# Cross attention on one core: output rows dealt over four steps, value chunks in a ring of four

## The reference, cut to what matters

```python
x = x + attn(layernorm(x))
h = layernorm(x)
q = (h @ Wq).reshape(B, 112, 16, 128)
k = (ctx @ Wk).reshape(B, 375, 8, 128)
v = (ctx @ Wv).reshape(B, 375, 8, 128)
p = softmax(where(mask, q k^T / sqrt(128), -inf))
x = x + (p v).reshape(B, 112, 2048) @ Wo
x = x + ffn(layernorm(x))
```

## Time and profile before

| | |
|---|---|
| Median of 3 runs | 2684.8 us (2684.68 to 2687.51) |
| The profiled execution | 2685.35 us, span 2683.7 us |
| TensorE matmuls (PE) | 2482.7 us busy, 93% |
| TensorE weight loads (PEld) | 2257.6 us, 84% |
| VectorE (DVE) | 1733.0 us, 65% |
| ScalarE (ACT) | 1241.2 us, 46% |
| GpSimd (POOL) | 1030.1 us, 38% |
| Mean granted TensorE clock | 0.957 |

### The profile page before, as it was taken

The page is one execution under the profiler, slowest core; times in us unless marked ns, Lnnn a source line. Parts: engine busy times, 40 slices in busy tenths (PEclk is TensorE's granted clock), DMA queues, the critical chain, the costliest instruction groups (busy, mean ns, idle before and its releaser), DMA issues. The chain is left out here.

```text
span 2683.7 us, 46237 instructions
## 1 busy us (share of the span) xinstructions
PE 2482.7 (93%) x14850; PEld 2257.6 (84%) x14851; DVE 1733.0 (65%) x4899; ACT 1241.2 (46%) x3183; POOL 1030.1 (38%) x1424
## 2 busy tenths in 40 slices
PE   6899897799999999999999999999999999979488
PEld 5888886788989898889989898898989888869376
DVE  7878886565575657566575756656565665644466
ACT  4555553454454545445454545445454454522211
POOL 4334443243343434334353534334343343431422
PEclk9999998899999999999999999999999999975699
DMA  8322332412122112212121211111111111122654
GB/s 256 95 71 84 96 108 89 162 50 66 62 75 66 62 54 74 74 52 83 52 91 58 88 55 53 54 41 55 51 57 54 53 55 41 41 72 70 220 178 129
DMA packets 108892, 217.87 MB, mean 81 GB/s; under 512 B 20336, under 2 KB 48720, under 8 KB 108416
## 3 DMA queue, kind: packets, MB, share of 16 engines
q1 hardware_dynamic: 103440, 188.42, 21.9%
q0 software_dynamic: 5040, 16.58, 1.7%
q10 hardware_dynamic: 224, 10.49, 1.2%
HBM read 134.57 MB, written 91.36 MB: 84 GB/s over the span
## 5 line engine op out<-in xcount | busy, mean ns | idle before, releaser
L1171 POOL TENSOR_SCALAR x_probs<-x_probs,x_inv 112x376 f32<-112x376 f32 x512 | 639.3, 1258 | 273.6 <-DVE x_inv L1323 273.6
L1165 POOL TENSOR_SCALAR x_bias<-x_top 112x1 f32<-112x1 f32 x512 | 129.1, 252 | 871.8 <-DVE x_top L1295 864.9
L1215 ACT ACTIVATE x_probs<-x_probs,x_bias 112x376 f32<-112x376 f32 x512 | 307.0, 603 | 105.2 <-POOL x_bias L1165 104.7
L1380 PE MATMUL x_ps_o<-x_pT,x_v 128*128 128x224 f32 (+1 forms) x2304 | 310.3, 279 | 43.2 <-DVE x_pT L1302 42.5
L1380 PEld LDWEIGHTS x_ps_o<-x_pT,x_v 128*128 128x128 f32 (+1 forms) x2304 | 288.0, 192 | 69.6 <-DVE x_pT L1302 61.5
L1380 PE MATMUL x_ps_f<-x_xT,x_wq 128*128 128x448 f32 x1536 | 339.3, 371 | 4.5 <-issue 4.5
L1380 PE MATMUL x_ps_f<-x_wo,x_oT 128*128 128x512 f32 x1344 | 315.7, 391 | 1.0 <-DVE x_oT L1311 1.0
L1380 PE MATMUL x_ps_s<-x_kT,x_qT 128*112 128x376 f32 x1536 | 314.6, 340 | 1.5 <-DVE x_top L1295 1.5
L1380 PE MATMUL x_ps_f<-x_ctxT,x_wk 128*128 128x376 f32 x1536 | 306.4, 335 | 1.9 <-DVE x_ctxT L1272 1.9
L1380 PEld LDWEIGHTS x_ps_f<-x_xT,x_wq 128*128 128x128 f32 x1536 | 282.4, 189 | 26.5 <-issue 4.7
L1380 PEld LDWEIGHTS x_ps_f<-x_wo,x_oT 128*128 128x128 f32 x1344 | 252.6, 189 | 50.0 <-issue 1.2
(11 more groups left out here) (186 smaller groups left out, 3799.5 us busy)
## 6 DMA issues: line engine op xcount, KB each, us to landing
x_ctxs<-x_ctxT SPq DMA_DIRECT2D x32, 752.0 KB, 3.8
x_ctxT<-x_ctxs SPq DMA_DIRECT2D x32, 752.0 KB, 4.3
x_xT<-h2T SPq DMA_DIRECT2D x16, 896.0 KB, 5.0
m_rows<-slots SPq DMA_DIRECT2D x35, 258.0 KB, 3.0
slots<-w_blank SPq DMA_DIRECT2D x8, 1032.0 KB, 5.2
x_ctxn<-in_ctx_dram SPq DMA_DIRECT2D x32, 256.0 KB
m_hn<-in_L_ffn_W_dram SPq DMA_DIRECT2D x32, 256.0 KB
w_xa<-in_x_dram SPq DMA_DIRECT2D x32, 224.0 KB, 3.3
```

What stands on the lines that cost most here:

```text
L1165: pool.tensor_scalar(bias[:, m:m + 1], top[:, m:m + 1], -0.1 * NEG, -SCALE, ALU.max, ALU.mult) \
L1171: pool.tensor_scalar(probs[0:T, m, 0:SE], probs[0:T, m, 0:SE], inv[:, m:m + 1], None, ALU.mult).then_inc(normed, 1)
L1215: act.activation(probs[0:T, m, 0:SE], probs[0:T, m, 0:SE], ACT.Exp, bias=bias[:, m:m + 1], scale=SCALE, accum_out=total[:, m:m + 1]).then_ ...
L1380: last = pe.matmul(out, w, r, start=m == 0, stop=m == len(jobs) - 1)
```

## The change

The output rows leave `ORDER`. They get a bank of their own, `ps_r`, taken from the fills, which now have two. A tile's eight heads are multiplied in four parts (`ROWS_AT`: 3, 1, 3 and 1 heads at g=2 and g=3 of the batch where the tile is due and at g=0 and g=1 of the next); VectorE adds the tile after the last part. `oT` holds three tiles instead of two. V's first chunk moves to g=3 of the batch before, which takes a ring of four chunk slots for `v`; the context of b+2 is transposed half at g=2, half at g=3, behind P·V. x pieces go to g=1 and g=2 of batches 1 and 2 of a quad. Weights of keys are kept for one half only, in pieces by head. The context as loaded and the raw mask have one buffer instead of two. On ScalarE and VectorE the exponentials and inverses now come ahead of the early fills, and mask row, x piece and weight piece go to the end of a step.

```diff
+    VRING = NKC + 1
...
-    RING = 2 * P
+    RING = 3 * P
...
-        out = [("K", b + 1, g)] if b + 1 < NB else []
-        if g == 3 and b + 2 < B:
-            out += [("C", b + 2, 0), ("C", b + 2, 1)]
-        if g == 2 and b in TILE_OF:
-            out.append(("O", TILE_OF[b], 0))
-        return out
+        return [("K", b + 1, g)] if b + 1 < NB else []
 
     def late_fills(i):
         b, g = divmod(i, G)
-        out = [("V", b, c) for c in range(NKC)] if g == 1 else []
+        out = []
+        if g >= 2 and b + 2 < B:
+            out.append(("C", b + 2, g - 2))
+        if g == 3 and b + 1 < NB:
+            out.append(("V", b + 1, 0))
+        if g == 1:
+            out += [("V", b, c) for c in range(1, NKC)]
         if b % QUAD == QUAD - 1 and b + 1 < NB:
             out += [("Q", b // QUAD + 1, 2 * g + h) for h in range(2)]
         return out
 
     def before_transposes(i):
-        return late_fills(i)[:-1]
+        fs = late_fills(i)
+        return fs if fs and fs[-1][0] == "C" else fs[:-1]
 
     def behind_transposes(i):
-        return late_fills(i)[-1:]
-
-    HEAD = [("C", 0, 0), ("C", 0, 1)] + [("K", 0, g) for g in range(G)] + [("C", 1, 0), ("C", 1, 1)] + \
-           [("Q", 0, h) for h in range(H)]
-    TAIL = ("O", TILE_OF[NB], 0)
-    ORDER = HEAD + [f for i in range(STEPS) for f in early_fills(i) + late_fills(i)] + [TAIL]
+        fs = late_fills(i)
+        return [] if fs and fs[-1][0] == "C" else fs[-1:]
+
+    ROWS_AT = {2: [(0, 3)], 3: [(3, 4)], 4: [(4, 7)], 5: [(7, H)]}
+
+    def row_parts(i):
+
+        out = []
+        for back in (1, 0):
+            b, g = divmod(i, G)
+            b, g = b - back, g + G * back
+            if b in TILE_OF:
+                out += [(TILE_OF[b], h0, h1) for h0, h1 in ROWS_AT.get(g, [])]
+                if b == NB - 1 and g == G - 1:
+                    out += [(TILE_OF[b], h0, h1) for late in ROWS_AT if late > g for h0, h1 in ROWS_AT[late]]
+        return out
+
+    HEAD = [("C", 0, 0), ("C", 0, 1)] + [("K", 0, g) for g in range(G)] + [("Q", 0, h) for h in range(4)] + \
+           [("C", 1, 0), ("C", 1, 1)] + [("Q", 0, h) for h in range(4, H)] + [("V", 0, 0)]
+    ORDER = HEAD + [f for i in range(STEPS) for f in early_fills(i) + late_fills(i)]
     PLACE = {f: n for n, f in enumerate(ORDER)}
     assert len(PLACE) == len(ORDER)
-    HALVED = {f: n for n, f in enumerate([f for f in ORDER if f[0] != "O"])}
-    BANKS = 3
+    BANKS = 2
...
-    PIECES = {"k": CC, "v": CC, "q": KC, "o": H // 2}
-    FIRST_SPLITS = [("k", 0, n) for n in range(CC)], [("q", 0, n) for n in range(KC)], [("v", 0, n) for n in range(CC)]
+    PIECES = {"k": G, "v": CC, "q": KC, "o": H // 2}
...
-        if b == B - 8 and g < CC:
-            return [("k", 1, g)]
+        if 0 <= i - G * (B - 2) - 1 < G:
+            return [("k", 1, i - G * (B - 2) - 1)]
         if b == B - 3:
             return [("q", 1, g)]
-        if i == G * B:
+        if i == G * (B - 1) + 2:
             return [("v", 1, n) for n in range(CC)]
-        if b == B + 1:
-            return [("o", 1, g)]
+        if 0 <= i - G * (B + 1) - 2 < PIECES["o"]:
+            return [("o", 1, i - G * (B + 1) - 2)]
...
-        return b // QUAD + 1 if b % QUAD == 1 and b // QUAD + 1 < NB // QUAD else None
+        if b // QUAD + 1 == NB // QUAD or b % QUAD not in (1, 2) or g not in (1, 2):
+            return None
+        return b // QUAD + 1, 2 * (b % QUAD - 1) + g - 1
...
+        def v_slot(b, c):
+            return (NKC * b + c) % VRING
...
                 for b in range(NB):
-                    if b + 2 < B:
-                        load_ctx(b + 2)
-                    if b + 1 < B:
-                        keep_ctxT(b + 1)
-                    if b + 1 in TILE_OF:
-                        load_base(TILE_OF[b + 1])
+                    if b in TILE_OF:
+                        load_base(TILE_OF[b])
                     if b % QUAD == 0 and b // QUAD + 1 < NB // QUAD:
                         load_x(b // QUAD + 1)
-                    if b == B - 12:
-                        for n in range(PIECES["k"]):
-                            load_w(("k", 1, n))
                     if b == B - 4:
                         sp.wait_ge(fill_ready, until(("Q", B // QUAD - 1, H - 1)))
                         for n in range(PIECES["q"]):
                             load_w(("q", 1, n))
+                    if B <= b + 2 < NB:
+                        load_ctxT(b + 2)
                     if b == B - 1:
                         sp.wait_ge(fill_ready, until(("V", B - 1, NKC - 1)))
                         for n in range(PIECES["v"]):
                             load_w(("v", 1, n))
-                    if B <= b + 2 < NB:
-                        load_ctxT(b + 2)
+                    if b - 1 in TILE_OF:
+                        store(TILE_OF[b - 1])
+                    if b == B + 1:
+                        sp.wait_ge(rows_ready, TILES)
+                        for n in range(PIECES["o"]):
+                            load_w(("o", 1, n))
                     if b + 2 < NB:
                         load_mask(b + 2)
-                    if b in TILE_OF:
-                        store(TILE_OF[b])
-                    if b == B:
-                        sp.wait_ge(fill_ready, until(("O", TILES - 1, 0)))
-                        for n in range(PIECES["o"]):
-                            load_w(("o", 1, n))
+                    if b == B - 2:
+                        for n in range(PIECES["k"]):
+                            sp.wait_ge(fill_ready, until(("K", B - 1, n)))
+                            load_w(("k", 1, n))
+                    if b + 2 < B:
+                        keep_ctxT(b + 2)
+                    if b + 3 < B:
+                        load_ctx(b + 3)
...
+                fill(HEAD[-1])
                 for i in range(STEPS):
-                    for p in splits_at(i):
-                        split(p)
+                    exps(i)
                     for f in early_fills(i):
-                        if f[0] != "O":
-                            fill(f)
-                    exps(i)
-                    if x_piece(i) is not None:
-                        split_x(x_piece(i), i % G)
+                        fill(f)
                     if i >= 2:
                         out(i - 2)
                     for f in before_transposes(i):
...
                         probsT(i - 1)
                     for f in behind_transposes(i):
                         fill(f)
+                    if x_piece(i) is not None:
+                        split_x(*x_piece(i))
+                    for p in splits_at(i):
+                        split(p)
...
+                mask_row(0)
                 for i in range(STEPS):
-                    if i % G == 0:
-                        mask_row(i // G)
                     maxima(i)
-                    for p in splits_at(i):
-                        split(p)
+                    inverses(i)
                     for f in early_fills(i):
-                        if f[0] != "O":
-                            fill(f)
-                    inverses(i)
-                    if x_piece(i) is not None:
-                        split_x(x_piece(i), i % G)
-                    for f in early_fills(i):
-                        if f[0] == "O":
-                            add(f)
+                        fill(f)
                     if i >= 2:
                         out(i - 2)
+                    for tile, h0, h1 in row_parts(i):
+                        if h1 == H:
+                            add(tile)
                     for f in before_transposes(i):
                         fill(f)
                     if i >= 1:
                         probsT(i - 1)
                     for f in behind_transposes(i):
                         fill(f)
+                    if i % G == 1 and i // G + 1 < NB:
+                        mask_row(i // G + 1)
+                    if x_piece(i) is not None:
+                        split_x(*x_piece(i))
+                    for p in splits_at(i):
+                        split(p)
...
+                def rows(tile, h0, h1):
+                    if h0 == 0:
+                        weights("o", tile // TILES)
+                        pe.wait_ge(o_lo, G * (last_batch(tile) + 1))
+                        if tile:
+                            pe.wait_ge(rows_added, tile)
+                    slot = tile * P % RING
+                    for h in range(h0, h1):
+                        for a, b_ in PASSES:
+                            last = pe.matmul(ps_r[:], oT[:, a, h, slot:slot + P], wo[:, b_, h, :],
+                                             start=h == 0 and (a, b_) == PASSES[0],
+                                             stop=h == H - 1 and (a, b_) == PASSES[-1])
+                    if h1 == H:
+                        last.then_inc(rows_ready, 1)
...
                     scores(i)
                     for f in early_fills(i):
                         fill(f)
```

(38 more changed lines are left out.)

69 lines of the change are left out of this document (38 added, 31 removed).

## The result

The changed kernel takes 2695.2 us (median of 6 runs, 2693.7 to 2699.7) against 2684.7 us for the kernel before, measured beside it: ratio 1.0041, 95% interval 1.0029 to 1.0054. It is slower, by 10.5 us; the forecast was 5 us faster. The time lies inside the range, the direction is wrong.

What follows compares the result with a forecast made beforehand. TensorE's instruction stream, working 97 to 99% of each quad, was taken as the bound. Head +6.3, first quad +2.9, other first-half quads +0.3 and second half −14.7 gave −5.2 us: forecast 2680 us, range 2655 to 2697.

Steps and rivals of the forecast that it cites:

- (g): First quad (four batches sharing one query set): VectorE bears four `wo` pieces in short steps; 117.0 against 114.1 us, +2.9.
- (b): Keys' low part behind inverses: stored 3.2 us after m, where maxima start; steps under 5.6 us cost up to 0.55.
- The first rival: New waits do not appear: about −3.2 us a full quad, −4 with a missing tile, near 2648; chance 0.20.
- (a): Step lengths with rows dealt over four steps: 24.7 us a first-half batch, 24.1 second-half; row parts cost 0.
- (d): Full quads: 120.4 against 121.9 us in the first half (−1.5), 116.3 against 119.0 in the second (−2.7).
- (e): Quads with a missing tile: first half 118.1 against 117.1 us (+1.0), second half 113.6 against 114.4 (−0.7).
- (f): Head, ahead of the first scores: first V chunk behind `wv`'s halving, second context between query products; +6.3 us.
- (h): Second-half key weights, one buffer, loaded in batch 30: ScalarE waits for a piece; +4.5 us once.
- (i): Second half's start and end: `wo` pieces in steps without rows 0; three batches without x −1.5, last batch −3 us.
- third rival: New idle times bring low-clock stretches, at most three or four of 1 to 1.5 us each: 2684; chance 0.08.

Runs made afterwards that it cites:

- chip 1: The kernel before and the changed kernel, both unaltered, run and traced again on another chip: changed kernel's ratio to the kernel before 1.0033.
- Pieces in the gap: The changed kernel, but VectorE halves each weight piece behind the next step's maxima instead of at the step's end: ratio to the kernel before 0.9999.
- all three placements: The changed kernel with `wo` loaded ahead of mask 1, second-half `wk` pieces halved one step later, VectorE's weight pieces behind the next maxima: ratio 0.9975.

## Why the prediction was wrong

**The failing step is (g), the first quad.** It was to cost +2.9 us and costs 8.7 on chip 1, which is 5.8 of the 12.6 us between forecast and measurement there, and 7.9 in the first profile. The miss is all in batch 0: 25 us worked out, 29.7 measured (30.4 on chip 1). The sum took VectorE to be busy without a break: four cycles of 4.2 us, the V halves, context, mask and pieces by their lengths. It left out what VectorE waits for. First, the loads were taken as landed, because the sentence on SyncE closed with "each is still issued most of a batch before its use … so nothing". That holds for the loads that the change moves and not for those queued behind them: dropping the second mask buffer puts a wait for mask row 0 ahead of four `wo` loads, and VectorE stands 3.1 us. Loading them first gives 1.0 to 2.9 us back. Second, a late key holds V2's bank, and VectorE then waits another 2.2 us for V2's product. Pieces in the gap give 3.7 to 5.6 us back, all three placements 6.6 on one chip, the keys' old order beside them another 8.2 (116.1 to 107.9), of which 4.0 are in batch 0. How the 5 to 6 us that were missed divide between the load, the bank and the low clock is not shown: the single edits overlap.

**(b) was worked out rightly.** "Keys stored at m + 3.2" (3.16) holds, and the short steps' 0.55 us stand in the 4.2 us of batch 0's four cycles. What it didn't ask is whether the new order is worth having. The first rival described the kernel with the old order back, roughly: −3.2 and −4 a quad, and 119.2 and 114.5 were measured (−2.7 and −2.5); "near 2648" is a ratio of 0.986, and that run had 0.9897. It said that earlier keys would do it, not that a change of order would bring them.

**(a), (d).** An unbroken first-half batch is 24.86 us, not 24.7, and V0's wait costs 0.54, not 0.65: full quads gained 0.8 us each, not 1.5. The row parts cost nothing, as taken. In the second half (d) and (e) were right to 0.3 us over six quads together. **(e)** in the first half came out at 118.2 to 118.4 for 118.1; it cost +1.3 a quad for +1.0, since the kernel before took 116.8 to 117.1 in these quads.

**(f)**, the head, cost +6.0 and +6.9 us from the first query product on, for 6.3. That the first scores also came 6.3 us later by the clock of chip 1 is luck, as the 10.7 of the first chip shows. **(h)**, ScalarE's wait for `wk`: 4.97 us for the "4 us or more", the quad +2.2 on chip 1 and +3.7 on the first for +1.8. **(i)**: of the −3 us at the end only 0.5 came on chip 1 (1.9 on the first), and quad 9, with `wo`'s pieces, cost 1.2 and 2.9 instead of nothing.

**The clock, third rival.** TensorE's busy time in the first quad rose from 107.9 us to 110.2, although it holds twelve matmuls of output rows fewer (36 for 48, 2.0 us of busy time), which now stand in the next quad: some 4 us of work more, an estimate, at the low clock behind the new idle times, on top of 5.6 us more of idling (11.8 against 6.2). The page "TensorE: Matmul & The Clock Gate" of the Trainium skill (Part 1) says that the throttled state is the default and activity releases it; by it the forecast would have been 4 us higher, and the trace agrees with its sign and size. This rival happened, but the longest of its idle times stood in part behind a load that none of the steps had.

In short: slower, because of two things that the forecast had half in hand, and mending either turns the sign. With the one-off work mended and nothing else the ratio is 0.9975; with the keys' order alone it is 0.9897.

## What to carry to other kernels

When a buffer is dropped, look at what is queued behind the load that now waits, not only at that load; here it was four weight loads in the same queue. Where two engines wait for each other in turn, the sum of one engine's lengths is a lower bound, and the one-off stretches are where that shows, since the steady state hides them from an average. A stretch that waits for a load varies from run to run (the unaltered first quad by 1.9 us), so an edit worth 1 to 3 us there needs its own chip's trace beside it. And the order of work that two engines hand over is one decision: undoing it on VectorE alone was 2.2% worse than undoing it on both, on ScalarE alone 1.3%.

## What the runs showed of the hardware

The repeating quads agree between two chips within 0.1 us, while the kernel's total differs by 14 us: the kernel before ends its cross attention at about 2395 us on both and has 288 us left on one and 274 on the other. So these two chips may be compared by quads of this kind, but not by totals.

After 5.19 us without a matmul six V matmuls took 2.91 us and six of the scores 2.08 (1.64 and 1.19 otherwise); after 2.65 us of waiting still 2.52 and 1.91; after 0.37 us nothing is seen. But the length of the wait doesn't settle it. V0 in g=3 of batch 0 has the same wait in several traces; in the first profile and on chip 1:

```profile
548.83 2.36 PE L1410 MATMUL x_ps_f<-x_wv,x_ctxT 128*128 128x512 f32 x6 [2.24 <-DVE x_kT L1302]
...
547.01 2.92 PE L1410 MATMUL x_ps_f<-x_wv,x_ctxT 128*128 128x512 f32 x6 [2.24 <-DVE x_kT L1302]
```

Behind 2.24 us the group took 2.36 and 2.92 us here, 1.73 in the run with the late `wk` pieces, and 2.93 behind 2.23 us in the one with `wo` loaded first.

The page "PSUM — Partial Sum Buffer" of the Trainium skill (Engine vs sequencer instructions) says that the queues of ScalarE and VectorE are strict first in, first out; VectorE's wait of 1.58 us for the keys' high part, with finished exponentials behind it, is what that costs when the two orders disagree.
